# Second attention of a gated two-layer block: batch 0's rows in a row, weight loads in order of use, and empty fills counted together

## What is computed

```
x = x + tanh(g_xattn[0]) * L0_xattn(ctx, layernorm(x), mask)      # heads over context and own rows
x = x + tanh(g_ffn[0])   * L0_ffn(layernorm(x), given experts)    # gelu experts
x = x + tanh(g_xattn[1]) * L1_xattn(layernorm(x), ctx)            # the second attention
x = x + tanh(g_ffn[1])   * L1_ffn(layernorm(x))                   # router softmax, top 2, swiglu experts

def L1_xattn(x, y):                    # 16 heads of 32
    q = (x @ wq + bq); k = (y @ wk + bk); v = (y @ wv + bv)       # split into heads
    attn = softmax(q k^T / sqrt(32))
    return (attn v) @ wo + bo
```

## Time and profile before

| | us |
|---|---|
| median of 3 runs | 4028.98 |
| lowest, highest | 4025.55, 4050.93 |
| the profiled execution, its own time | 4035.9 |
| its span in the trace | 4034.1 |

### The profile page before, as it was taken

The page is one execution under the profiler, slowest core; times in us unless marked ns, Lnnn a source line. Parts: engine busy times, 40 slices in busy tenths (PEclk is TensorE's granted clock), DMA queues, the critical chain, the costliest instruction groups (busy, mean ns, idle before and its releaser), DMA issues. The chain is left out here.

```text
span 4034.1 us, 62650 instructions
## 1 busy us (share of the span) xinstructions
PE 3717.7 (92%) x21848; PEld 2940.4 (73%) x21848; DVE 2914.3 (72%) x4500; ACT 1904.2 (47%) x2703; POOL 1063.2 (26%) x990
## 2 busy tenths in 40 slices
PE   7899999999789999999958999759999999999998
PEld 4555666556478898989935555459988898889897
DVE  5576766666668787877627887577887777777785
ACT  2555655555445555554415445214444444444443
POOL 2222221122011111111035654213233323333331
PEclk9999999999899999999979999769999999999999
DMA  4100000000167777776431221137777767776774
GB/s 157 31 29 18 26 31 32 31 26 9 71 228 247 275 252 265 265 248 208 161 113 42 85 76 49 44 104 222 218 224 227 230 202 220 226 227 207 216 237 124
DMA packets 386020, 595.28 MB, mean 148 GB/s; under 512 B 26127, under 2 KB 192079, under 8 KB 385551
## 3 DMA queue, kind: packets, MB, share of 16 engines
q1 hardware_dynamic: 352575, 521.68, 38.6%
q0 software_dynamic: 23856, 56.15, 6.3%
q10 hardware_dynamic: 9368, 14.33, 1.0%
HBM read 532.96 MB, written 59.12 MB: 147 GB/s over the span
## 5 line engine op out<-in xcount | busy, mean ns | idle before, releaser
L1409 PE MATMUL bank<-e_xh,e_WH 128*128 128x256 f32 x1984 | 572.3, 288 | 38.8 <-issue 32.6
L1250 DVE TENSOR_TENSOR e_all<-e_all_raw,e_WH 128x2048 fp32r<-128x2048 f32 x240 | 547.3, 2289 | 67.8 <-ACT e_WH L1244 67.1
L1409 PE MATMUL bank<-e_xl,e_WH 128*128 128x256 f32 x1984 | 570.4, 288 | 0.0
L1409 PE MATMUL bank<-e_xh,e_all 128*128 128x256 f32 x1984 | 570.1, 287 | 0.0
L1244 ACT ACTIVATE e_WH<-e_all_raw 128x2048 fp32r<-128x2048 f32 x240 | 458.3, 1910 | 221.7 <-DMA e_all_raw<-in_w 221.7
L1462 PE MATMUL bank<-e_WH,e_hh 128*128 128x512 f32 x1192 | 474.2, 398 | 0.0
L1462 PE MATMUL bank<-e_WH,e_hl 128*128 128x512 f32 x1192 | 468.3, 393 | 0.0
L1409 PEld LDWEIGHTS bank<-e_xh,e_WH 128*128 128x128 f32 x1984 | 387.7, 195 | 44.0 <-issue 42.1
L1409 PEld LDWEIGHTS bank<-e_xl,e_WH 128*128 128x128 f32 x1984 | 387.7, 195 | 0.9
L1409 PEld LDWEIGHTS bank<-e_xh,e_all 128*128 128x128 f32 x1984 | 387.3, 195 | 0.0
L1485 ACT ACTIVATE e_sil<-bank 128x256 f32<-128x256 f32 x248 | 95.3, 384 | 398.9 <-PE bank L1409 398.9
(11 more groups left out here) (380 smaller groups left out, 9206.2 us busy)
## 6 DMA issues: line engine op xcount, KB each, us to landing
e_all_raw<-in_w SPq DMA_DIRECT2D x320, 512.0 KB, 4.6
f_wl_raw<-in_w SPq DMA_DIRECT2D x120, 1024.0 KB, 5.6
e_all_raw<-in_w SPq DMA_DIRECT2D x80, 1024.0 KB, 5.3
e_rest_raw<-in_w SPq DMA_DIRECT2D x72, 1024.0 KB, 5.5
f_X<-in_x SPq DMA_DIRECT2D x32, 256.0 KB, 2.7
f_R<-in_x SPq DMA_DIRECT2D x32, 256.0 KB, 4.4
x<-f_R SPq DMA_DIRECT2D x32, 256.0 KB, 2.0
a_X<-x SPq DMA_DIRECT2D x32, 256.0 KB, 3.4
```

The lines of the kernel that those rows point to most:

```text
L1250: dve.tensor_tensor(self.WL(p), self.raw(p), self.WH(p).bitcast(F32), ALU.subtract).then_inc(self.w_ready.sem, 1)
L1409: mm = nc.tensor.matmul(up[n % RING][:, q * ROWS:q * ROWS + ROWS], w, xx[:, c, :], start=(c == 0 and i == 0), stop=(c == DC - 1 and i == 2))
```

## The change

In both attentions a fill of no batch now issues nothing: `do` counts it for its bank, and the next real fill of that bank waits for what the real fills before it gave back, then adds the count to both semaphores with one instruction each, and goes on. In `attention1`, moreover:

- GpSimd and VectorE do bias, statistics, root and norm of all four tiles of batch 0 first, ahead of the bodies; the tables then leave batch 0 out.
- `w_in` becomes `wq_in` (wq, bq) and `wo_in` (wo, gw, bo). TensorE and ScalarE no longer wait for weights at the start; each q fill waits for `wq_in`, each o fill on TensorE for `wo_in`.
- SyncE's order becomes bf, X of batch 0, wq, bq, kT, X of batch 1, V, bv, wo, gw, bo.
- The gate on bo moves from body -1 to body 0.

```diff
@@ attention0 and attention1, do of the tensor engine (the same in both)
+                left_out = [0, 0]
+
                 def do(n, f):
...
                     bk_, c_ = fill(i, f)
-                    if c_ > 1:
-                        pe.wait_ge(emptied[bk_], c_ - 1)
                     if not there(n, f):
-                        pe.sem_inc(filled[bk_], 1)
-                        pe.sem_inc(emptied[bk_], 1)
+                        left_out[bk_] += 1
                         return
+                    if c_ - 1 > left_out[bk_]:
+                        pe.wait_ge(emptied[bk_], c_ - 1 - left_out[bk_])
+                    if left_out[bk_]:
+                        pe.sem_inc(filled[bk_], left_out[bk_])
+                        pe.sem_inc(emptied[bk_], left_out[bk_])
+                        left_out[bk_] = 0
...
                     elif kind == "q":
+                        pe.wait_ge(wq_in, 32)
...
                     elif kind == "o":
+                        pe.wait_ge(wo_in, 48)
@@ attention1, sync
                 load_x(0)
-                for dst, src in ((wq, "wq1"), (wo, "wo1"), (gw, "gw1")):
-                    sp.dma_start(dst[:, :, :], ins[src].rearrange("(c p) n -> p c n", p=P)).then_inc(w_in, 16)
-                sp.dma_start(bq[:, :], ins["bq1"]).then_inc(w_in, 16)
-                sp.dma_start(bo[:, :], ins["bo1"][None, :].to_broadcast([P, D])).then_inc(w_in, 16)
+                sp.dma_start(wq[:, :, :], ins["wq1"].rearrange("(c p) n -> p c n", p=P)).then_inc(wq_in, 16)
+                sp.dma_start(bq[:, :], ins["bq1"]).then_inc(wq_in, 16)
+                sp.dma_start(kT[:, :, :], k.kT1).then_inc(kv_in, 16)
+                load_x(1)
+                sp.dma_start(V[:, :, :], k.V1).then_inc(kv_in, 16)
                 sp.dma_start(bv[:, :], ins["bv1"]).then_inc(kv_in, 16)
-                sp.dma_start(kT[:, :, :], k.kT1).then_inc(kv_in, 16)
-                sp.dma_start(V[:, :, :], k.V1).then_inc(kv_in, 16)
+                for dst, src in ((wo, "wo1"), (gw, "gw1")):
+                    sp.dma_start(dst[:, :, :], ins[src].rearrange("(c p) n -> p c n", p=P)).then_inc(wo_in, 16)
+                sp.dma_start(bo[:, :], ins["bo1"][None, :].to_broadcast([P, D])).then_inc(wo_in, 16)
...
-                    if -2 <= n < B - 3:
+                    if -1 <= n < B - 3:
                         load_x(n + 3)
@@ attention1, gpsimd
+                for t in range(QT + 1):
+                    if t < QT:
+                        bias(0, t)
+                    if t:
+                        root(0, t - 1)
                 for n in bodies:
-                    if n == -1:
-                        pool.wait_ge(w_in, 16 * 5)
+                    if n == 0:
+                        pool.wait_ge(wo_in, 48)
...
-                        if s in ROOT1_AT and 0 <= n + ROOT1_AT[s][0] < B:
+                        if s in ROOT1_AT and 0 < n + ROOT1_AT[s][0] < B:
...
-                        if s in BIAS1_AT and 0 <= n + BIAS1_AT[s][0] < B:
+                        if s in BIAS1_AT and 0 < n + BIAS1_AT[s][0] < B:
@@ attention1, tensor and scalar
-                pe.wait_ge(w_in, 16 * 5)
...
-                act.wait_ge(w_in, 16 * 5)
...
                     elif kind == "q":
+                        act.wait_ge(wq_in, 32)
                         x = act.activation(qT[:, a, :], m, ACT.Identity, bias=bq[:, a:a + 1])
@@ attention1, vector
+                for t in range(QT + 1):
+                    if t < QT:
+                        add(0, t)
+                    if t:
+                        norm(0, t - 1)
                 for n in bodies:
...
-                        if s in NORM1_AT and 0 <= n + NORM1_AT[s][0] < B:
+                        if s in NORM1_AT and 0 < n + NORM1_AT[s][0] < B:
...
-                        if s in ADD_AT and 0 <= n + ADD_AT[s][0] < B:
+                        if s in ADD_AT and 0 < n + ADD_AT[s][0] < B:
```

More of the change, by code:

```diff
@@ L526, in do @@
                     bk, n = fill(b, f)
-                    if n > 1:
-                        pe.wait_ge(emptied[bk], n - 1)
                     if not there(b, f):
-                        pe.sem_inc(filled[bk], 1)
-                        pe.sem_inc(emptied[bk], 1)
+                        left_out[bk] += 1
                         return
+                    if n - 1 > left_out[bk]:
+                        pe.wait_ge(emptied[bk], n - 1 - left_out[bk])
+                    if left_out[bk]:
+                        pe.sem_inc(filled[bk], left_out[bk])
+                        pe.sem_inc(emptied[bk], left_out[bk])
+                        left_out[bk] = 0
                     m, rows = mb[bk], rows_of(t)
@@ L1664, in attention1 @@
         chunks = lambda bk_: bk_.rearrange("p (c n) -> p c n", c=DC)
-        w_in, kv_in, bf_in, folded, kzeroed = sem("weights_in"), sem("kv_in"), sem("bf_in"), sem("folded"), sem("kzeroed")
+        wq_in, wo_in, kv_in, bf_in, folded, kzeroed = \
+            sem("wq_in"), sem("wo_in"), sem("kv_in"), sem("bf_in"), sem("folded"), sem("kzeroed")
         k_ready = sem("k_ready")
```

## The result

Four runs of the changed kernel took 3981.66 us in the median (3981.21 to 3982.57), four of the kernel before 4031.44 (4025.55 to 4050.93): ratio 0.9871, 95% interval 0.9848 to 0.9894. The change is worth 1.3%, where the forecast was 0.9%.

A forecast was written before the change was run, and what follows sets the result against it. TensorE is busiest, kept full by the experts; the change targets its idle stretches at the two attentions' edges. Terms -10.5 - 19.9 - 7.0 + 0.5 = -36.9 from 4028.98 give 3992 us; 8-in-10 range 3981 to 4006.

The forecast's parts named there:

- The price of a fill: A fill of no batch, one wait and two increments on TensorE's sequencer, costs 0.317 us.
- part 4: Waits added to q and o fills in the second attention: +0.5 us, bounds 0 and +6.8.
- Rival 1: Gaps at both attentions' ends are barrier and semaphore clearing, fills cost next to nothing: 4006 us; chance 0.1.
- rival 4: 64 added waits open bubbles in the second attention, lowering the clock more often: 4046 us at 0.82; chance 0.03.
- Part 1: End of the first attention: fills -8.5, clock staying up -1.0, other bodies -1.0; sum -10.5 us.
- Part 2: Head of the second attention: first scores 19.9 us earlier, low clock +2.5, bodies 0 and 1 -2.5; sum -19.9.
- Rival 3: Second attention's head: V, bv or wo land later, or bo's fold holds GpSimd: 3997 to 3999 us; chance 0.17.
- Rival 2: Second attention's head: V loads at 397 GB/s, stops ending last, no gap lowers the clock: 3986 us; chance 0.15.
- The low clock behind the gap (+2.5): Second attention's head: after TensorE stands still, first scores and q2 run partly at low clock; bounds 0 and +4.8.
- Bodies 0 and 1: Second attention: gaps from 14 and 3 fills of no batch shrink, -2.5 us, bounds 0 and -5.
- Part 3: End of the second attention: -5.4 us in the gap before the routing, -1.6 ahead of it; sum -7.0.
- The chain of the last tiles: Near the second attention's end, three gaps holding fills of no batch go: -1.6 us.

The follow-up runs named there:

- fills_first_only: The kernel before, with only the first attention's fills of no batch counted together; 4019.91 us, ratio 0.9974.
- old_load_order: The changed kernel with the second attention's loads back in their old order; 3985.5 us, ratio to before 0.9899.
- fills_second_only: The kernel before, with only the second attention's fills of no batch counted together; 4005.16 us, ratio 0.9938.
- rows_loads_only: The changed kernel with the old single fills of no batch in both attentions; 4017.04 us, ratio to before 0.9973.
- single_at_start: The changed kernel with the second attention's fills of no batch single again before body 4 only; 3991.04 us, ratio to before 0.9912.
- single_at_end: The changed kernel with the second attention's fills of no batch single again from body 4 on only; 3991.9 us, ratio to before 0.9915.

## Why the prediction was right or wrong

- **The price of a fill**: right at 0.317 against 0.306 (two increments) and 0.293 (7.9 / 27). The three rows it came from were good ones. Wrong was what it is made of: part 4 bounded an added wait at a third of it, 0.106, and 64 at +6.8; 27 waits cost 0.06 us. The value taken, +0.5, was near nothing, and so is the measurement. Rival 1 is refuted by both ends, rival 4 by the granted clock between the eleventh and the last centring: 0.97 in both kernels. (The 0.94 of rows 2 had the half clock of body 8 in it, which stands behind the last centring.)
- **Part 1**, -10.5: the fills gave -7.9 of -8.5. The clock (-1.0) gave nothing: the gap was short and the first matmul quick, and it fell a microsecond later. Bodies 7, -1 and 0 (-1.0) gave nothing in this execution; fills_first_only shows another 1.6 before its end and 2.2 in its head, as much as traces of the same code differ: with the same first attention the first experts start between 1120.98 and 1123.58 us, and the head of the kernel before, 53.1 us from the memset to the first scores, takes 51.3 and 50.5 with 54 and 108 increments far ahead of it.
- **Part 2**, -19.9: the first scores came 21.6 us earlier. V landed 26.9 us after the memset (2039.24 + 20.5), not 29.7; bv 1.3 us behind V, and that, not V, released the keys. Rival 3 did not come. Rival 2 came in part: its sign, not its mechanism, for V still took 20.5 us and the stretch in which it loads moves 220 and 183 GB/s. The low clock behind the gap (+2.5) did not come here, but did in old_load_order, where the first scores take 1.39 us and q2 behind them 5.05.
- **Bodies 0 and 1**, the term most under-sized by its own kind: -2.5 against -5.3 with no loss to set against it. From the first scores to the eleventh centring fills_second_only gains 4.5, and rows_loads_only loses 2.4 by the new order; in that order the same fills cost more, 6.9 in single_at_start (8.3 less the 1.4 before the first scores) and 7.7 against rows_loads_only, which less 2.4 is the 5.3. I had let the softmax chain hide half of them.
- **Part 3**, -7.0: the gap gave 5.2 of 5.4. The chain of the last tiles gave 3.8 where I had 1.6 (single_at_end; 3.6 against the execution with 54). Behind its gap of 1.46 us a transposition takes 1.09 us, against 0.63, so part of it is the low clock; whether the gap brings that on is not shown.
- **The step that failed** is the term of part 3 for the chain of the last tiles, -1.6, which put the clock of bodies 8 and 9 at nothing: "Sum -7.0; bounds -1 and -8" left no room for it, since I read the mean of 0.94 over 400 us as the stage's constant. These bodies gave 12.1 us. 8.6 of them are the half clock of body 8 in the execution profiled before, which the traces with counted fills do not show; 3.6 are the chain. Why the clock falls there is open. The second step was to let the softmax chain hide half of the fills in bodies 0 and 1.
- **The base.** I summed from the median. The profiled execution before lay 6.9 above it, and part of body 8's 8.6 us may be in that; the change of medians is 49.8 us (47.2 by the 24 runs). Forecast less gained, in the order of the table, is +2.6, -1.7, -5.3, +0.2, -10.5, +0.2 and -2.2, together -16.7, and 36.9 + 16.7 makes the 53.6 of the spans.
- **The chances**: the forecast 3992 stood 3.3 us inside "within 1%" (3988.7), and the time came out 7 us beyond it. The range held by 0.7 us, and that is luck: its lower end is called rival 2 with a bound of part 1 on top, but the bounds of part 1 add up to 13.6, 3.1 more than its 10.5, so 3986 less that is 3983 and not 3981, and by that end the time lies outside. Rival 2 at 3986 and the forecast's own range, 3986 to 3998, both missed it; none had a term for the clock of a stretch that comes and goes.

## What to carry to other kernels

On a sequencer that ends last, count increments, not waits: each bare increment of TensorE cost 0.153 us here and 27 satisfied waits 0.06 together, so placeholders in a hand-written order should be counted and credited in one. Read the granted clock in windows of 20 us or so over the whole stage that is touched, in several executions: a mean hides a stretch at half clock that comes and goes. And before believing that a part has cost something, look whether it was lost where the part is; here 24.4 us were lost in a loop whose first pause came 340 us behind the end of the changed code.

## What the runs showed of the hardware that I had not expected

- Increments on TensorE's sequencer take 0.153 us each where nothing hides them (8.27 and 8.28 us for 54), and 27 satisfied waits 0.06 together. In the changed kernel 54 cost 3.2 us; that the other 5 lay beside matmuls still running is argued.
- The granted clock falls for a few us again and again in the second attention (windows of 6 us in the changed kernel: 0.67 and 0.76 at 2276 and 2282, 0.72 at 2342, 0.69 and 0.74 at 2402 and 2408), and in some executions for some 20 us in body 8, with the same instructions: 8.6 us.
- V (1.97 MB, 120 partitions) takes 20.5 us from issue to landing, at 183 to 220 GB/s, where the loads ahead of it move 390; it took 19.2 and 21.3 in the two other orders of the loads. Why is open.
- Seven pauses of about 3.0 us behind the first matmul of a loop's group came in one kernel and went with 64 instructions added ahead of the loop: 24.4 us over the stage.
